# One-tile-a-partition dispatch tables, regions emptied ahead, interleaved scatters and a third result buffer in a macaron block (two MoE layers around attention)

## The reference, cut to what matters

```python
# x: (4, 512, 256), 2048 tokens; the same FFN weights are used twice
x = x + 0.5 * ffn(layernorm(x))
x = x + attention(layernorm(x))          # 16 heads of 128, softmax over 512 keys
x = x + 0.5 * ffn(layernorm(x))

def ffn(h):                              # 16 experts, top 2, F_EXP = 128, F_SH = 256
    flat = h.reshape(-1, 256)
    router_logits = flat @ router_w.T
    topk_w, topk_idx = top_k(softmax(router_logits), 2)      # weights normalized to sum 1
    shared = silu(flat @ shared_gate_w) * (flat @ shared_up_w) @ shared_down_w
    # tokens sorted by expert, one gate/up/down product an expert (ragged_dot)
    dn = (silu(xs @ gate_w[e]) * (xs @ up_w[e])) @ down_w[e]
    return shared + scatter_add(weight * dn)
```

## Time and profile before

| | |
|---|---|
| median of 3 runs | 1249.88 us (1244.11 to 1250.19) |
| the profiled execution | 1238.46 us |
| its span on the core | 1236.7 us |
| PE, DVE, ACT, POOL busy | 90%, 69%, 58%, 30% of the span |
| mean granted TensorE clock | 0.963 of full speed |

### The profile page before, as it was taken

One profiled execution on the slowest core, in us unless ns is written; L12 is line 12 of the kernel. 1 busy time (PEld: TensorE's weight loads), 2 busy tenths in 40 slices (PEclk: granted clock), 3 DMA queues, 4 the chain that ended last, 5 costly groups with the idle time before them and its releaser, 6 DMA issues.

```text
span 1236.7 us, 20720 instructions
## 1 busy us (share of the span) xinstructions
PE 1108.0 (90%) x6360; PEld 957.0 (77%) x6360; DVE 856.8 (69%) x1837; ACT 719.2 (58%) x1485; POOL 372.7 (30%) x458
## 2 busy tenths in 40 slices
PE   5759984799999999999999999999999999858994
PEld 5648873687888878888888888888888877747884
DVE  7455436788777787877778777787777777653336
ACT  5226432666766766767767676676767666424441
POOL 2714567220003463400154320124001042342550
PEclk9869997899999999999999999999999999978997
DMA  4546435020013104400022430011000012655425
GB/s 172 186 151 185 139 102 165 10 69 1 1 54 118 41 24 153 129 5 1 18 65 87 144 95 1 9 35 53 1 1 1 2 62 105 236 171 144 135 81 204
DMA packets 58602, 103.76 MB, mean 84 GB/s; under 512 B 12756, under 2 KB 41819, under 8 KB 57952
## 3 DMA queue, kind: packets, MB, share of 16 engines
q1 hardware_dynamic: 50816, 85.60, 22.2%
q0 software_dynamic: 7680, 16.84, 3.8%
HBM read 70.89 MB, written 40.16 MB: 90 GB/s over the span
## 4 chain that ended last, share of the span: by engine, by line
PE 75%; DVE 7%; issue 6%; ACT 4%; DMA 3%; SPq 2%; another core or an unknown queue 2%; POOL 1%; POOLq 0%; DVEq 0%; ACTq 0%
PE bank L1327 14%; PE bank L1329 14%; PE bank L1328 14%; PE bank L1546 9%; PE bank L1554 5%; PE bank L1556 4%; PE bank L1555 4%; PE bank L1573 2%; PE bank L1572 2%; PE bank L1571 2%; PE bank L1418 1%; DMA y_dram<-work 1%; PE bank L1338 1%; POOL y_dram L502 1%
## 5 line engine op out<-in xcount | busy, mean ns | idle before, releaser
L1327 PE MATMUL bank<-R 128*128 128x512 f32 (+2 forms) x1056 | 405.0, 384 | 57.9 <-DVE X L996 21.3
L1328 PE MATMUL bank<-R 128*128 128x512 f32 (+2 forms) x1056 | 382.1, 362 | 0.0
L1329 PE MATMUL bank<-R 128*128 128x512 f32 (+2 forms) x1056 | 381.4, 361 | 0.0
L1327 PEld LDWEIGHTS bank<-R 128*128 128x128 f32 x1056 | 207.1, 196 | 99.0 <-issue 46.7
L1329 PEld LDWEIGHTS bank<-R 128*128 128x128 f32 x1056 | 206.7, 196 | 28.8
L1328 PEld LDWEIGHTS bank<-R 128*128 128x128 f32 x1056 | 207.7, 197 | 22.3
L1142 DVE TENSOR_REDUCE mx<-bank 128x1 f32<-128x512 f32 x256 | 174.5, 691 | 61.0 <-PE bank L1329 59.3
L736 ACT ACTIVATE work<-bank,mx 128x512 f32<-128x512 f32 x256 | 175.4, 690 | 59.2 <-DVE mx L1142 58.4
L1135 DVE SCALAR_TENSOR_TENSOR R<-bank,bias,R 128x512 fp32r<-128x512 f32 x192 | 143.7, 748 | 71.9 <-ACT R L730 70.5
L747 ACT ACTIVATE R<-bank 128x512 fp32r<-128x512 f32 x256 | 139.2, 598 | 65.9 <-PE bank L1546 65.7
L1155 DVE TENSOR_TENSOR R<-bank,R 128x512 fp32r<-128x512 f32 x256 | 167.6, 679 | 1.8 <-ACT R L747 1.0
(11 more groups left out here) (125 smaller groups left out, 1549.7 us busy)
## 6 DMA issues: line engine op xcount, KB each, us to landing
work<-in_ffn_w SPq DMA_DIRECT2D x34, 384.0 KB, 4.6
work<-xs_dram SPq DMA_DIRECT2D x96, 128.5 KB
w_dram<-work SPq DMA_DIRECT2D x16, 768.0 KB, 4.0
R<-w_dram SPq DMA_DIRECT2D x16, 768.0 KB
work<-in_codes SPq DMA_DIRECT2D x64, 128.0 KB
work<-in_scales SPq DMA_DIRECT2D x256, 32.0 KB
R<-y_dram SPq DMA_DIRECT2D x10, 512.0 KB, 7.2
xs_dram<-in_empty SPq DMA_DIRECT2D x34, 128.5 KB, 3.1
```

Of the source, the lines that this page charges most:

```text
L1327: nc.tensor.matmul(out, ah, bh, start=(i == 0 and first), stop=False)
L1328: nc.tensor.matmul(out, ah, bl, start=False, stop=False)
L1329: last = nc.tensor.matmul(out, al, bh, start=False, stop=(i == n - 1))
```

## The change

1. **Tables.** `tables` now works on all 128 partitions, tile i on partition i (`counts` leaves the counts on every partition). Two small matmuls on PE (`tables_row`) turn the columns into one row, and DVE copies it out as `toff` and `words`. PE loads `words` into registers (`tile_words`) before its last early `down`.
2. **Empty rows.** In layer 1 whole regions are written empty, in 17 DMAs (17 rows a partition, 2.2 MB each) between the loads of attention weights; `fills(1)` is gone. In layer 0 `fills` reads its rows from SBUF and is issued in one go.
3. **Scatters.** All tiles are marked once at the start of layer 0; the choice 0 scatters of batch q+1 come ahead of the choice 1 scatters of batch q. In layer 1 the last two batches have a second copy of their rows (`rows_2`), so that choice 1 needs no wait.
4. **Results.** RESULTS = 3 buffers in `m.dnb`; the product h is written over the silu.
5. **Around them.** 9 chunks instead of 11 are loaded ahead of the tiles, and two chunks are split in each of the first two pairs; router `logits` run by halves of D, each as its low part is ready; `shared_h(0, 7)` comes before the combination of batch 0; in layer 1 the tables come before `shared_h(1, 0)`; the first `TENSOR_LOAD` of `toff` takes 2 registers instead of 8.

```diff
-PRE_CHUNKS = 11
+PRE_CHUNKS = 9
+WITH_PAIR = (2, 2, 1, 1, 1, 1, 1)
+CHUNK_AT = {2: 9, 3: 10, 4: 11, 6: 12, 8: 13, 10: 14, 12: 15, 14: 16, 15: 17}
+RESULTS = 3
+GROUPS = (2, 6) + 5 * (8,)
...
+    def empty_region(e):
+        r0, r1 = e * REGION, min((e + 1) * REGION, XROWS)
+        rows = m.xs_dram[1][r0:r1, :].rearrange("(p a) d -> p (a d)", p=P)
+        sp.dma_start(rows, t["empty"][:, 0:(r1 - r0) // P * ROW]).then_inc(s["empty"], 16)
...
         for n in range(g * PARTS_G + (HG if g == 1 else 0), (g + 1) * PARTS_G):
             part(n)
+            e = (n - PARTS_G - HG) // 2
+            if n % 2 and e <= NE:
+                empty_region(e)
...
-    f1 = fills(1)
-    for _ in range(FILLS_FIRST[1] + 1):
-        next(f1, None)
-    tile_loads(1, f1)
+    tile_loads(1)
...
     pool.wait_ge(s["cst_in"], 48)
-    for q in range(QB):
-        scatter(0, q)
+    marked(m.rows, 0, slice(0, NT))
+    scatter_first(0)
+    for q in range(1, QB):
+        scatter_first(q)
+        scatter_second(q - 1)
+    scatter_second(QB - 1)
     results(0)
...
                 for j in range(2):
-                    wait(act, m.res[2 * b + j], RES_F * f + 16 * ((p - 2) // 2))
-                nc.scalar.activation(m.dnb[:, b, :], bank[6 + b][:], ACT.Copy).then_inc(s["r_ev"], 1)
+                    wait(act, m.res[2 * b + j], RES_F * f + 16 * ((p - 2) // RESULTS))
+                nc.scalar.activation(m.dnb[:, b], bank[6 + p % 2][:], ACT.Copy).then_inc(s["r_ev"], 1)
...
     def tables(f):
-        te, off = m.te[:, 0, :], m.te[:, 1, :]
-        n = NR // 2
-        for i in range(2):
...
+        te, off = m.tt[:, 0:1], m.tt[:, 1:2]
...
+        st.link(v_.tensor_scalar(taken, cum, c1[:, C_T:C_T + 1], None, ALU.is_le))
+        st.did(v_.reduce_sum(m.tt[:, 2:3], taken, AX_X))
+        st.link(v_.tensor_tensor(cum, taken, gap, ALU.mult))
+        st.did(v_.reduce_sum(m.tt[:, 3:4], cum, AX_X))
...
+    def tables_row(f):                       # PE
+        pe.wait_ge(s[f"tt{f}"], 1)
+        nc.tensor.matmul(bank[2][0:1, at:at + NR], m.tt[:, 1:2], row[:, 0:NR], start=True, stop=True)
+        nc.tensor.matmul(bank[2][0:1, at + NR:TABLE[1]], m.tt[:, 0:1], row[:, NR:], start=True, stop=True)
```

More of the change, by code:

```diff
@@ L333, in tile_loads @@
+    def tile_loads(f):
         sp.wait_ge(s[f"toff{f}"], 1)
[L334 to L337, removed]
+        if f == 0:
+            sp.wait_ge(s["fill0"], 16 * NE)
+        for name in ("scat_a", "scat_b"):
+            sp.wait_ge(s[name], 16 * 2 * QB * (f + 1))
         sp.wait_ge(s["scat_2"], 16 * NT * (f + 1))
-        for i0 in range(0, NR, 8):
+        i0 = 0
+        for group in GROUPS:
@@ L340, in tile_loads @@
             _, at = nc.values_load_multi_w_load_instructions(
[L341 to L347, removed]
+                m.toff[0:1, i0:i0 + group], engines=[SP_ENGINE], min_val=0, max_val=XROWS - P)
@@ L380, in presplit_out @@
         sp.dma_start(m.w_dram[e], m.pre_w.rearrange("p l n -> p (l n)")).then_inc(s["pre_out"], 16)
-    for c in range(STAGES, 9):
+    for c in range(STAGES, PRE_CHUNKS):
         chunk(c)
-    f0 = fills(0)
-    for _ in range(FILLS_FIRST[0] + 1):
-        next(f0, None)
-    for c in range(9, PRE_CHUNKS):
-        chunk(c)
-    tile_loads(0, f0)
+    fills()
+    tile_loads(0)
     for n in range(4):
@@ new lines, in marked, with first_of, to_experts @@
+    def marked(rows, k, tiles):
+        nc.gpsimd.tensor_copy(rows[:, :, D:ROW].bitcast(I32), m.target[:, k, tiles].unsqueeze(2)).then_inc(s["meta"], 1)
+        metas[0] += 1
+        pool.wait_ge(s["meta"], metas[0])
+    def first_of(q):
+        return s[("scat_a", "scat_b")[q % 2]]
+    def to_experts(f, q, k, rows, sem):
+        for i in range(QB):
+            n = QB * q + i
+            nc.gpsimd.indirect_dma_start(
+                out=m.xs_dram[f], out_offset=bass.IndirectOffsetOnAxis(ap=m.pos[:, k, n:n + 1], axis=0),
+                in_=rows[:, i, :], in_offset=None).then_inc(sem, 16)
@@ L1090, in dve_program @@
     positions(0, 3, K0)
-    free_rows(0, CNT)
+    counted(0, CNT)
+    free_rows()
+    tables(0)
     split_lo(1)
     shared_h(0, 0)
-    tables_expert()
+    tables_row(0)
     shared_h(0, 1)
-    shared_h(0, 2)
-    tables(0)
-    shared_h(0, 3)
-    shared_add(0, 0)
-    for step in range(2, EARLY[0]):
+    for step in range(1, EARLY[0]):
         shared_h(0, 2 * step)
+        shared_add(0, step - 1)
         shared_h(0, 2 * step + 1)
-        shared_add(0, step - 1)
     split_lo(PRE_CHUNKS - 6)
@@ L1108, in dve_program @@
     xna = lambda b: m.xna[:, b % 2]
-    for k in range(2 * EARLY[0], 2 * QB - 1):
-        shared_h(0, k)
+    for step in range(EARLY[0], QB):
+        shared_h(0, 2 * step)
+        if step > EARLY[0]:
+            shared_add(0, step - 1)
+        shared_h(0, 2 * step + 1)
     choice_weights(0)
@@ L1119, in dve_program @@
     normalize("a", 0, xna(0), (0, 1))
-    for step in range(EARLY[0], QB):
-        shared_add(0, step)
     combine_half(1, 0)
@@ L1263, in dve_program @@
             statistics(ph, q)
+    positions(1, 2, K0)
     y_add(UNITS // 4 - 1)
@@ L1274, in dve_program @@
     xt_los("1", 3, 2)
-    shared_h(1, 0)
     choose(1, 3, L0)
     positions(1, 3, K0)
-    free_rows(1, CNT)
+    counted(1, CNT)
+    tables(1)
+    shared_h(1, 0)
+    tables_row(1)
     shared_h(1, 1)
-    tables_expert()
-    tables(1)
     choice_weights(1)
@@ L1708, in pe_program @@
     pe.wait_ge(s["e_in"], 16 * NE)
-    tiles(1)
+    tiles(1, word)
     shared_late(1)
```

277 lines of the change are left out of this document (152 added, 125 removed), and 4 rows, old and new, of the table SEMAPHORES.

## The result

Slower: 1258.09 us (median of 15 runs) against 1244.11 us for the kernel before, run beside it (15 runs). The ratio is 1.0103, with a 95% interval of 1.0078 to 1.0129. I had forecast 1214 us, 35.5 less than the median of three runs of before, 1249.88; counted from 1244.11 the same sum gives 1209. Another measurement of the same two kernels further down has a ratio of 0.9995 (0.9966 to 1.0024), so what holds in both is that the change brought no gain; the 1% of loss was met once. The profiled execution has a span of 1256.5 us, 19.8 more than before's 1236.7.

What follows compares the result with a forecast made beforehand. PE, busy for 90% of the span, bounds the kernel, so only its idle stretches can give: 11.5 + 10 + 5 - 1 + 0 + 10 + 0 = 35.5 us, from 1249.88 to 1214, range 1199 to 1228.

Steps and rivals of the forecast that it cites:

- The third buffer: Tiles of both layers: evictions no longer wait for landings, PE becomes the bound at 2.81 us a pair; 10 us gained each.
- first rival: Tiles stay slower than PE through longer landings, late tile loads or another cause of silu's wait; 1223 or 1234 us, chance 0.22.
- the cycle of eviction, scatter and landing on one buffer: Tiles before the change: this cycle, not POOL, was taken as the limit, at 3.56 us a pair against 2.81 unblocked.
- First dispatch: Start of layer 0: scatters, fills and tables end sooner, first transpose at 72.5 instead of 83.96; 11.5 us gained, bounds 6 and 15.
- positions don't hold it: First dispatch: batch 3 is scattered from about 46 on, behind its positions at 43.63 + 0.29.
- the 63 of the sum: First dispatch: POOL's scatters, with no wait for landings, end at 63 against 67.67 before.
- Chunks in layer 0: First tiles of layer 0: tile 6 behind chunk 12 on SP; 2 us of stall, counted inside the layer's 10.
- Passage: From layer 0's tiles to attention: shared_h(0, 7) earlier, first projection at 206 instead of 211.68; 5 us gained, 3 to 6.
- Attention: 17 region writes, 109 us of full load in all, delay weight parts without PE seeing it; 1 us charged, at most 9.
- second rival: Region writes disturb attention at the upper bound of 9 us; 1222 us, chance 0.13.
- the slower one by its mechanism: Attention: region writes delay weight parts until PE waits, 4 us for each of 16 regions; 1277 us, chance 0.04.
- Second dispatch: Start of layer 1: rows come sooner but PE's own chain decides, gate product at 1118.70 moves by 0; bounds 3 either way.

Runs made afterwards that it cites:

- exact_wait: Changed kernel, with each tile load waiting for the result of the tile 16 before, whose place it takes; ratio to before 0.9968.
- split_first: Changed kernel, with ACT's part of the weight splits ahead of the normalization again, as before the change; ratio to before 1.0175.
- pause: Changed kernel, with POOL waiting for PE's counts before it scatters the second choice of batch 1; ratio to before 1.0214.
- series 1: First series of follow-up runs: four single edits of the changed kernel, with the kernel before beside them at 1203.5 us.
- changed_again: The changed kernel as it is, run again beside the kernel before at 1255.2 us; ratio 0.9995.
- exact_order: Changed kernel with the edits of exact_wait and split_first together; ratio to before 0.9893.
- no_rows_b: Second run of exact_chunks with result scatters that carry hardly a row, POOL issuing as many; 1241 us, before at 1258.3.
- exact_chunks: exact_order with the weight chunks loaded as before the change; ratio to before 0.9837.
- rests_regs: exact_chunks with three POOL rests for PE's signals in the first dispatch, and SP reading registers ahead of its waits; 1235.25 us, ratio 0.9819.

## Why the prediction was wrong

**The third buffer (forecast: -10 us a layer; measured: +10 and +8).** Three steps failed. First, that the tile loads "wait for transposes and landings of 16 tiles before" I took over from the old code, without working the changed index through. Where no signal is late it is the larger part of the loss: exact_wait against split_first and pause is worth about 2% in series 1. Where signals are late, as in the measurement that I forecast, it weighs less: between changed_again and exact_order layer 0 goes from 101.8 to 99.6 us and layer 1 from 86.3 to 84.1, some 2 us a layer. In the first measurement, where layer 1 grew by 8 us, its share stays open between the two. Late tile loads stood among the conditions of my first rival, but priced only as a gain not made. Second, "the cycle of eviction, scatter and landing on one buffer is" the limit was false, and with it the gain of 10 us a layer. The coincidence of 4.14 us in the earlier trace rows misled me: with three buffers and the exact wait the same rhythm of 3.6 us stays where signals are late, and with two buffers it is 2.8 where they aren't. The silu of the earlier trace rows, whose 3.62 us I could not explain, was the key. PE had ended the product that it waits for at 154.25, 2.6 us before the silu's start at 156.87:

```profile
153.97 0.28 PE L1329 MATMUL bank<-R 128*128 x1
```

It starts 0.83 us behind the end of the scatter at 155.06, as in no_rows_b. So the third, "POOL itself idles 2.26 us in each round, so it isn't the limit", failed as well: POOL sets the rhythm not by its busy time but by four scatters in a row. That wait stood in my own rows and spoke against the main term.

**First dispatch (forecast -11.5 to 72.5; measured +5.5, 89.4).** That "positions don't hold it" failed, at batch 1 and not at batch 3: POOL idled 5.26 us for the positions of batch 1 and ended its scatters at 67.18, 4 us behind the 63 of the sum. The first scatter of batch 3 stands at 51.28, 1.1 us behind its positions, without a wait. I had not priced ACT's two moved splits (the 2.9 us twice on DVE; 4 us at the first transposes in series 1). The late signals in front of counts and gate products I did not foresee, though in before the copy of the counts is 2.4 us late too. And I took the fills to start by 50 without looking at what stands ahead of them on SP: chunk 8, whose split now follows the tables. But of the 20 us by which the fills are late chunk 8 explains at most 3: in exact_wait, with the same order and no late signal, they start at 52.75. Where no signal is late the head is 71 to 75 us, with the scatters' end at 66 to 69 and not at 63.

**Chunks in layer 0 (2 us).** Mis-sized: 22.7 to 24.2 us for the first five steps, instead of 15.6 to 20.4 in the runs with the chunks as before; 7 us between exact_order and exact_chunks. SP stands behind chunk 12 until the split of chunk 9.

**Passage (-5).** Right in kind, 2.5 us in size; 32 to 37 us in the other runs of the changed code, against 38.2.

**Attention (+1).** Nothing: 859.92 us, and between 859 and 862 in every run. The region writes (16 of 2.24 MB and a small one) raised the DMA share from 0.16 to 0.28, which is 103 us of full load in place of the 109 of my sum, and cost no time, so the second rival and the slower one by its mechanism are both refuted. It became slower by another, to which I had given no chance of its own.

**Second dispatch (0) and tail (0).** -1.6 and about +1 us.

**What stays open.** What makes the two conditions differ: the same chip number showed both. What in POOL's issuing holds PE's signals, and slows SP beside them; in the first dispatch of the changed kernel the counts came through at 57.98 in the midst of scatters. The traces of the runs with late signals also lack some 20 to 50 of PE's 1100 semaphore records, the others at most three; whether the recording itself has a part in the delay, no run shows. And the changed kernel itself was not run in the condition of 1203 us; that it is some 2% slower there is read from split_first and pause.

## What to carry to other kernels

When a count of buffers or semaphores changes, work every index and every modulus that uses it through for three or four tiles by hand, in the waits of the other queues too: here 16 divides by 4 and not by 6, and a third of the waits asked for a result four tiles too new, the others for one two tiles too old. Ahead of a sum that rests on what ends a wait, explain every idle time in the same round; one that names no releaser is the first thing to settle, not a remark. And where work is moved behind something on one engine, follow it through the other engines that are in step with it (here ACT's split, DVE's split, the chunk, the fills).

## What the runs showed of the hardware

PE's signals can be seen late while POOL issues indirect transfers without rest: 2.8 us late behind four scatters of 0.98 us with gaps of 0.30, and in the first dispatch, where POOL ran for some 45 us with little rest, from 2 us (the counts in exact_order) to 26 us (in exact_chunks). In the tiles they come through 0.83 to 0.95 us behind the end of a run of scatters, and those still held at the end of the first dispatch 1.8 to 2.2 us behind its last scatter (after, exact_chunks, rests_regs). SP is slower in such a stretch too: 7.4 us for reading eight registers, against 3.1 in exact_wait. Nearly empty scatters do it too (3.6 us a pair), half as many don't (2.8 us). In the series where before took 1203 us the same code showed no such delay, even with POOL busy for 42.20 of 67.33 us.

The Trainium skill (TensorE: Matmul & The Clock Gate, The cost: per-tile semaphore tail) has the increments of small packed matmuls line up, at some 26 ns for each. No run here packs matmuls so; the 0.02 us of split_first is of that order, and the 2.8 us of no_rows_b is a hundred times as much, and there the measurement decides.
